# Dense attention in two-head groups with two-bank score tiles, instead of four-head groups with one-bank tiles

## The chip, the cores and the metric

One Trainium2 chip, all 8 of its cores. Every core runs the same program on its own batch element (one 2048 x 1024 slice of x). The time is the device time of the slowest core, in microseconds. There is no exchange between cores.

## What is computed

A transformer block in two halves, each wrapped in layer norms with a residual. The change touches only the first half, a dense (all keys) attention with 16 heads of 64 over 2048 tokens:

```python
def _L0_attn_ref(x, qkv_w, qkv_b, proj_w, proj_b):      # x: (8, 2048, 1024)
    qkv = einsum('bsd,ed->bse', x, qkv_w) + qkv_b        # 16 heads of 64
    scores = einsum('bhqe,bhke->bhqk', q, k) / sqrt(64)
    attn = softmax(scores, axis=-1)
    out = einsum('bhqk,bhke->bhqe', attn, v)
    return einsum('bsd,ed->bse', out, proj_w) + proj_b

x = x + layernorm(_L0_attn_ref(layernorm(x), ...))
x = x + layernorm(_L0_ffn_ref(layernorm(x), ...))       # two layers: windowed attention, gated FFN
```

The second half (two layers of windowed attention with rotary embedding and a gated feed-forward net) is the same before and after.

## The kernel before

The kernel is a chain of phases. Within a phase each engine has its instruction list in program order, written out by hand; a helper, `Phase.op`, attaches the semaphore waits. It adds one more wait to every VectorE instruction (for the VectorE instruction before it) and the same on ScalarE, so that neither engine ever overlaps two of its own instructions. A barrier stands between phases.

Phase D0 takes the layer-norm statistics, D1 makes the keys `kT` (bf16, head pair c on partitions 0-63 and 64-127) and the values `vTM` (bf16, keys on partitions, with a column of ones at index 64 that yields the softmax sums), D2 makes queries, attention and output projection. D2 runs four times, once for each block of 512 queries (`qb`). In each it computes the queries `qto` (L549, L554), a bound on each head's scores as the negative number to add before the exponential (L569 to L584), then the attention proper (L588 to L672), then the normalisation (L673 to L694), the projection (L699 to L724) and the statistics and residual (L729 to L788).

The attention proper, which is what the change rewrites, goes over four groups `cg` of two head pairs each (four heads). Of each group:

- L603 spreads the bound of each of the four heads over 128 partitions with a small matmul, L606 copies it to SBUF (`bnegb`, in the buffer that the profile calls sqbuf), one copy for each head.
- The loop `kc` runs over 16 chunks of 128 keys, and one step more. In step kc, L623 computes four score tiles (one for each head; 64 rows of the array each, 128 keys x 512 queries), each into its own PSUM bank 0 to 3; L630 adds the bound and writes `tmp2` (f32, one slot for each head); L637 takes the exponential into `pt` (bf16, two slots for each head, by the parity of kc). Then L653 multiplies the values of chunk ka = kc-1 with `pt`, four matmuls with 65 output rows, accumulated in PSUM banks 4 to 7.
- L661 to L670 evict the two sums and the two outputs of each head pair, eight VectorE instructions for the group.

Three waits matter. L623 waits for the add of the step before on its bank. L630 waits for the exponential of the step before on its `tmp2` slot. And L653 waits for `s_exp[bank]`: the dictionary holds the exponential last issued for that bank, and when L653 of chunk kc-1 is issued, step kc has overwritten it. So L653 of chunk kc-1 waits for the exponential of chunk kc. TensorE issues in order, so the score matmuls of step kc+1 stand behind those.

## Time and profile before

| | before |
|---|---|
| median of 2 runs | 5703.12 us (5676.47 to 5729.78) |
| profiled execution, its own time | 5702.29 us |
| its span, slowest core (core 5) | 5700.7 us |
| spans of the eight cores | 5654.3 to 5700.7 us |
| TensorE busy | 3448.1 us, 60% |
| VectorE busy | 2057.9 us, 36% |
| ScalarE busy | 1457.4 us, 26% |
| GpSimd busy | 200.3 us, 4% |

The span is the time from the first to the last instruction of the slowest core. Busy shares are means over the whole span, and phases differ much from one another; no engine is near full. A group of instructions is one source line on one engine: its busy time, the mean duration of one, and the idle time of that engine directly before them, with what ended it. The granted clock is the share of TensorE's full 2.4 GHz that was passed to it: 0.50 is 1.2 GHz.

### The profile page before, as it was taken

The page shows a single profiled execution, that of the slowest core. Times are in us where ns is not written, and L with a number is a line of the kernel's source. Part 1 is how long each engine was busy: PE and PEld are TensorE (multiplying, and loading weights), DVE is VectorE, ACT ScalarE, POOL GpSimd, SP SyncE. Part 2 cuts the span into 40 slices and gives each one's busy share as a digit, 9 for nine tenths or more (in the row PEclk, how much of TensorE's full clock was granted, in tenths as well). Part 3 has the DMA queues.
Part 4 walks back from the last instruction along what each step waited for, and adds up shares of the span by engine and source line. Part 5 has one row for each costly group of instructions (what it writes and reads, how often), then busy time and mean ns, then how long its engine had stood idle before and what let it go on. Part 6 is the DMA issues. An engine that isn't in the chain of part 4 may idle for free. (4 is left out here: it accounts for less than half of the span.)

```text
span 5700.7 us, 45607 instructions; the slowest of 8 cores (5654.3 to 5700.7 us)
## 1 busy us (share of the span) xinstructions
PE 3448.1 (60%) x10688; PEld 1058.7 (19%) x10688; DVE 2057.9 (36%) x2871; ACT 1457.4 (26%) x2325; POOL 200.3 (4%) x211
## 2 busy tenths in 40 slices
PE   2656664565466556641555756969654774788891
PEld 0211111111111111110111211424211111133330
DVE  2112553455255345534333334222033333322215
ACT  2222442343244334421122222111021221311211
POOL 0000000000000000000000000101000000011010
PEclk8786556555655555555666565989766556599895
DMA  3001001100300110022000000635600000045453
GB/s 91 1 0 19 1 1 16 15 1 1 30 1 1 15 15 1 1 70 59 1 1 1 1 1 12 79 41 73 99 0 0 1 1 0 8 59 63 54 62 118
DMA packets 268634, 143.96 MB, mean 25 GB/s; under 512 B 161728, under 2 KB 251968, under 8 KB 265312
## 3 DMA queue, kind: packets, MB, share of 16 engines
q0 software_dynamic: 256144, 107.27, 15.5%
q1 hardware_dynamic: 12240, 33.78, 1.7%
q8 instruction: 106, 1.74, 0.1%
q14 instruction: 144, 1.18, 0.1%
HBM read 222.99 MB, written 16.78 MB: 42 GB/s over the span
## 5 line engine op out<-in xcount | busy, mean ns | idle before, releaser
L630 DVE TENSOR_TENSOR tmp<-psD,sqbuf 128x512 f32<-128x512 f32 x1024 | 708.4, 692 | 626.9 <-PE psD L623 540.9
L653 PE MATMUL psD<-PTbuf,vTM 128*65 128x512 bf16 x1024 | 610.3, 609 | 497.9 <-ACT PTbuf L637 491.4
L637 ACT ACTIVATE PTbuf<-tmp 128x512 bf16<-128x512 f32 x1024 | 646.1, 631 | 823.6 <-DVE tmp L630 698.7
L1175 PE MATMUL psF<-xhat,w1b 128*128 128x512 bf16 x1408 | 341.5, 386 | 66.6 <-DVE xhat L1149 60.3
L623 PE MATMUL psD<-qTO,kT 64*128 64x512 bf16 x1024 | 306.2, 613 | 75.2 <-DVE sqbuf L606 61.1
L885 PE MATMUL psA<-castbuf,wkv 128*128 128x512 bf16 x768 | 256.2, 493 | 156.9 <-DVE castbuf L866 133.8
L1181 PE MATMUL psF<-xhat,w1b 128*128 128x512 bf16 x1408 | 336.9, 383 | 0.0
L1216 PE MATMUL psF<-Gbuf,w2b 128*128 128x512 bf16 x1408 | 325.5, 396 | 15.1 <-DVE Gbuf L1191 8.1
L653 PEld LDWEIGHTS psD<-PTbuf,vTM 128*65 128x65 bf16 x1024 | 136.6, 133 | 1055.1 <-issue 1055.0
L1191 DVE SCALAR_TENSOR_TENSOR Gbuf<-psF,s_b1i,gel 128x512 bf16<-128x512 f32 x176 | 132.1, 751 | 506.6 <-ACT gel L1188 506.6
L1022 ACT ACTIVATE PTA<-psA,s_cf 128x512 bf16<-128x512 f32 (+1 forms) x448 | 236.8, 528 | 287.1 <-PE psA L1010 269.7
L1005 PE MATMUL psA<-qv,kb 64*128 64x512 bf16 x448 | 270.7, 604 | 4.4 <-DVE vTMl L974 4.4
L1188 ACT ACTIVATE gel<-psF,s_b1i 128x512 bf16<-128x512 f32 x176 | 121.1, 688 | 484.5 <-PE psF L1181 484.5
L1046 PE MATMUL psA<-PTA,vTMl 128*65 128x512 bf16 x448 | 233.7, 631 | 12.1 <-DVE PTA L1029 7.3
L1029 DVE MEMSET PTA<- 128x128 bf16 (+1 forms) x336 | 91.3, 272 | 316.9 <-PE psA L1046 277.5
L1175 PEld LDWEIGHTS psF<-xhat,w1b 128*128 128x128 bf16 x1408 | 136.4, 99 | 245.4 <-issue 100.7
L1216 PEld LDWEIGHTS psF<-Gbuf,w2b 128*128 128x128 bf16 x1408 | 141.6, 101 | 199.0 <-issue 79.3
L1181 PEld LDWEIGHTS psF<-xhat,w1b 128*128 128x128 bf16 x1408 | 139.0, 99 | 170.5 <-issue 12.2
L68 POOL DMA_DIRECT2D w1b<-w1i x88 | 83.8, 953 | 2462.0 <-SPq L79 1749.8
L549 PE MATMUL psD<-castbuf,wQ 128*128 128x512 bf16 x256 | 83.1, 492 | 132.0 <-DVE castbuf L521 90.7
L1222 DVE SCALAR_TENSOR_TENSOR x_res<-psF,s_b,x_res 128x512 f32<-128x512 f32 x64 | 48.1, 752 | 288.6 <-PE psF L1216 288.6
L951 PE MATMUL psA<-u2b,c_rr 128*128 128x512 bf16 x64 | 37.5, 585 | 171.0 <-DVE u2b L949 171.0
(204 smaller groups left out, 2996.2 us busy)
## 6 DMA issues: line engine op xcount, KB each, us to landing
w1b<-w1i POOLq DMA_DIRECT2D x88, 512.0 KB, 6.0
w2b<-w2p POOLq DMA_DIRECT2D x32, 704.0 KB, 8.3
x_res<-xT SPq DMA_DIRECT2D x1, 8192.0 KB, 29.2
wQ<-wqT POOLq DMA_DIRECT2D x32, 256.0 KB, 4.5
wP<-projT POOLq DMA_DIRECT2D x32, 256.0 KB, 4.6
xsave<-x_res SPq DMA_DIRECT2D x1, 8192.0 KB, 25.3
xo<-xsave SPq DMA_DIRECT2D x4, 2048.0 KB, 12.7
yT<-tmpo SPq DMA_DIRECT2D x4, 2048.0 KB
```

The lines of the kernel that those rows point to most:

```text
L623: tmm = ph.op("tensor", lambda e, kc=kc, r0=r0, bank=bank, cc=cc: e.matmul(pb[:, bank, :], kT[r0:r0 + 64, cc, kc * 128:kc * 128 + 128], qt ...
L630: v_add[bank] = ph.op("vector", lambda e, bank=bank, bslot=bslot: e.tensor_tensor(tmp2[:, bank, :], pb[:, bank, :], bnegb[:, bslot, :], AL ...
L637: s_exp[bank] = ph.op("scalar", lambda e, slot=slot, bank=bank: e.activation(pt[:, slot, :], tmp2[:, bank, :], AF.Exp, scale=0.125), waits ...
L653: t_av[slot] = ph.op("tensor", lambda e, cc=cc, ka=ka, slot=slot, obank=obank, par_h=par_h: e.matmul(pb[0:65, obank, :], vTM[:, ka, 2 * cc ...
L885: tlast = ph.op("tensor", lambda e, ci=ci, par=par, co=co, sl=sl: e.matmul(pb[:, par, :], wkv[:, ci, co * 128:co * 128 + 128], sl, start=( ...
L1005: ph.op("tensor", lambda e, c=c, kt=kt, r0=r0, bank=bank: e.matmul(pb[:, bank, :], kb[r0:r0 + 64, c, kt * 128:kt * 128 + 128], qv[r0:r0 + ...
L1022: s_exp[bank] = ph.op("scalar", lambda e, bank=bank, e0=e0, e1=e1: e.activation(pt[:, bank, e0:e1], pb[:, bank, e0:e1], AF.Exp, bias=b.s_c ...
L1046: t_av[bank] = ph.op("tensor", lambda e, c=c, kt=kt_a, bank=bank, obank=obase + par_h, par_h=par_h, ka=ka, nk=nk: e.matmul(pb[0:65, obank, ...
L1175: tl_a = ph.op("tensor", lambda e, ci=ci, jp=jp, bA=bA, o=o: e.matmul(pb[:, bA, :], w1b[:, jp, ci, 0:128], xh[:, ci, o:o + QB], start=(ci ...
L1181: tl_g = ph.op("tensor", lambda e, ci=ci, jp=jp, bG=bG, o=o: e.matmul(pb[:, bG, :], w1b[:, jp, ci, 128:256], xh[:, ci, o:o + QB], start=(c ...
L1191: v_g[sg] = ph.op("vector", lambda e, bA=bA, j=j, o=o, s_g=s_g, sg=sg: e.scalar_tensor_tensor(G[:, j, o:o + QB], pb[:, bA, :], b.s_b1i[:, ...
L1216: tl = ph.op("tensor", lambda e, j=j, fp=fp, bank=bank, o=o: e.matmul(pb[:, bank, :], w2b[:, fp, j, :], G[:, j, o:o + QB], start=(j == 0), ...
```

## The change

The loops of the attention proper are rewritten; all that is around them stays. The group is now one head pair c (eight groups for a query block instead of four). A step `kg` takes two chunks of keys of both heads. The four PSUM score banks are now given by head and chunk (bank = 2*par_h + j2) and not by head alone; the four matmuls of a step are issued as head 0 chunk 0, head 0 chunk 1, head 1 chunk 0, head 1 chunk 1. One add and one exponential serve two banks, 128 x 1024 elements, with the bound broadcast over the two. The value matmuls of step kg-1 now wait for the exponentials recorded under step kg-1. Output banks are 4, 5 for even c and 6, 7 for odd c. A wait of `kg == 0` and the list that ScalarE waits for at L737 are written for the new names.

The core of the diff (the evictions and the normalisation that follow are the same statements with `cc` renamed to `c`):

```diff
@@ -587,89 +587,92 @@
                 inc="V")
             v_oev = None
             v_last_of_pair = {}
-            s_exp = {0: None, 1: None, 2: None, 3: None}
-            v_add = {0: None, 1: None, 2: None, 3: None}
-            v_bb = {0: None, 1: None, 2: None, 3: None}
+            s_expg = {}
+            v_addg = {}
+            v_bb = {}
             t_av = {i: 0 for i in range(8)}
-            for cg in range(4):
-                pairs = (2 * cg, 2 * cg + 1)
-                for cc in pairs:
-                    for par_h in range(2):
-                        h = 2 * cc + par_h
-                        bslot = (cc % 2) * 2 + par_h
-                        wts = [("V", v_bq)]
-                        if v_add[bslot] is not None:
-                            wts.append(("V", v_add[bslot]))
-                        t_s = ph.op("tensor", lambda e, h=h, bslot=bslot: e.matmul(
-                            pb[:, bslot, :], b.c_selh[:, h * 128:h * 128 + 128],
-                            bq16[:], start=True, stop=True), waits=wts, inc="T")
-                        v_bb[bslot] = ph.op("vector", lambda e, bslot=bslot: e.tensor_copy(
-                            bnegb[:, bslot, :], pb[:, bslot, :]), waits=[("T", t_s)], inc="V")
+            for c in range(8):
+                obase = 4 + 2 * (c % 2)
+                for par_h in range(2):
+                    h = 2 * c + par_h
+                    bslot = (c % 2) * 2 + par_h
+                    wts = [("V", v_bq)]
+                    if v_addg.get((7, par_h, c - 1)) is not None:
+                        wts.append(("V", v_addg[(7, par_h, c - 1)]))
+                    t_s = ph.op("tensor", lambda e, h=h, par_h=par_h: e.matmul(
+                        pb[:, par_h * 2, :], b.c_selh[:, h * 128:h * 128 + 128],
+                        bq16[:], start=True, stop=True), waits=wts, inc="T")
+                    v_bb[bslot] = ph.op("vector", lambda e, bslot=bslot, par_h=par_h: e.tensor_copy(
+                        bnegb[:, bslot, :], pb[:, par_h * 2, :]), waits=[("T", t_s)], inc="V")
                 t_avl = {}
-                for kc in range(17):
-                    if kc < 16:
-                        for cc in pairs:
-                            for par_h in range(2):
-                                bank = (cc % 2) * 2 + par_h
-                                bslot = bank
-                                r0 = 64 * par_h
+                for kg in range(9):
+                    if kg < 8:
+                        tsm = {}
+                        for par_h in range(2):
+                            for j2 in range(2):
+                                kc = 2 * kg + j2
+                                bank = par_h * 2 + j2
                                 waits = []
-                                if s_evq[0] is not None and kc == 0 and par_h == 0 and cc == pairs[0]:
+                                if s_evq[0] is not None and kg == 0 and par_h == 0 and j2 == 0:
                                     waits += [("S", s_evq[0]), ("S", s_evq[1])]
-                                if v_add[bank] is not None:
-                                    waits.append(("V", v_add[bank]))
-                                if kc == 0:
-                                    waits.append(("V", v_bb[bslot]))
-                                tmm = ph.op("tensor", lambda e, kc=kc, r0=r0, bank=bank, cc=cc: e.matmul(
-                                    pb[:, bank, :], kT[r0:r0 + 64, cc, kc * 128:kc * 128 + 128],
-                                    qto[r0:r0 + 64, cc, :], start=True, stop=True,
+                                prev_add = v_addg.get((kg - 1, par_h, c)) or v_addg.get((7, par_h, c - 1))
+                                if kg == 0:
+                                    waits.append(("V", v_bb[(c % 2) * 2 + par_h]))
+                                if prev_add is not None:
+                                    waits.append(("V", prev_add))
+                                tsm[par_h] = ph.op("tensor", lambda e, kc=kc, r0=64 * par_h, bank=bank, c=c: e.matmul(
+                                    pb[:, bank, :], kT[r0:r0 + 64, c, kc * 128:kc * 128 + 128],
+                                    qto[r0:r0 + 64, c, :], start=True, stop=True,
                                     tile_position=(r0, 0)), waits=waits, inc="T")
-                                aw2 = [("T", tmm)]
-                                if s_exp[bank] is not None:
-                                    aw2.append(("S", s_exp[bank]))
-                                v_add[bank] = ph.op("vector", lambda e, bank=bank, bslot=bslot: e.tensor_tensor(
-                                    tmp2[:, bank, :], pb[:, bank, :], bnegb[:, bslot, :],
-                                    ALU.add), waits=aw2, inc="V")
-                                slot = bank + 4 * (kc % 2)
-                                wts = [("V", v_add[bank])]
-                                if t_av[slot]:
-                                    wts.append(("T", t_av[slot]))
-                                s_exp[bank] = ph.op("scalar", lambda e, slot=slot, bank=bank: e.activation(
-                                    pt[:, slot, :], tmp2[:, bank, :], AF.Exp,
-                                    scale=0.125), waits=wts, inc="S")
-                    if kc >= 1:
-                        ka = kc - 1
-                        for cc in pairs:
-                            for par_h in range(2):
-                                bank = (cc % 2) * 2 + par_h
-                                obank = 4 + bank
-                                avw = [("S", s_exp[bank])]
+                        for par_h in range(2):
+                            bslot = (c % 2) * 2 + par_h
+                            aw = [("T", tsm[par_h])]
+                            prev_exp = s_expg.get((kg - 1, par_h, c)) or s_expg.get((7, par_h, c - 1))
+                            if prev_exp is not None:
+                                aw.append(("S", prev_exp))
+                            v_addg[(kg, par_h, c)] = ph.op("vector", lambda e, par_h=par_h, bslot=bslot: e.tensor_tensor(
+                                tmp2[:, par_h * 2:par_h * 2 + 2, :],
+                                pb[:, par_h * 2:par_h * 2 + 2, :],
+                                bnegb[:, bslot:bslot + 1, :].broadcast_to([128, 2, QB]),
+                                ALU.add), waits=aw, inc="V")
+                            ptbase = (kg % 2) * 4 + par_h * 2
+                            wts = [("V", v_addg[(kg, par_h, c)])]
+                            if t_av[ptbase] or t_av[ptbase + 1]:
+                                wts.append(("T", max(t_av[ptbase], t_av[ptbase + 1])))
+                            s_expg[(kg, par_h, c)] = ph.op("scalar", lambda e, par_h=par_h, ptbase=ptbase: e.activation(
+                                pt[:, ptbase:ptbase + 2, :], tmp2[:, par_h * 2:par_h * 2 + 2, :],
+                                AF.Exp, scale=0.125), waits=wts, inc="S")
+                    if kg >= 1:
+                        kga = kg - 1
+                        for par_h in range(2):
+                            for j2 in range(2):
+                                ka = 2 * kga + j2
+                                slot = (kga % 2) * 4 + par_h * 2 + j2
+                                obank = obase + par_h
+                                avw = [("S", s_expg[(kga, par_h, c)])]
                                 if ka == 0:
-                                    if v_last_of_pair.get(cc - 2) is not None:
-                                        avw.append(("V", v_last_of_pair[cc - 2]))
-                                    if cc % 2 == 1 and s_qn_prev and cg == 0:
+                                    if v_last_of_pair.get(c - 2) is not None:
+                                        avw.append(("V", v_last_of_pair[c - 2]))
+                                    if c == 1 and s_qn_prev:
                                         avw.append(("S", s_qn_prev))
-                                slot = bank + 4 * (ka % 2)
-                                t_av[slot] = ph.op("tensor", lambda e, cc=cc, ka=ka, slot=slot, obank=obank, par_h=par_h: e.matmul(
-                                    pb[0:65, obank, :], vTM[:, ka, 2 * cc + par_h, 0:65],
+                                t_av[slot] = ph.op("tensor", lambda e, c=c, ka=ka, slot=slot, obank=obank, par_h=par_h: e.matmul(
+                                    pb[0:65, obank, :], vTM[:, ka, 2 * c + par_h, 0:65],
                                     pt[:, slot, :], start=(ka == 0), stop=(ka == 15)),
                                     waits=avw, inc="T")
-                                t_avl[(cc, par_h)] = t_av[slot]
...
@@ -731,9 +734,10 @@
                 sqw2 = []
                 if c == 0:
                     sqw2 = [("S", s_att[0]), ("S", s_att[1])]
-                    for bk in range(4):
-                        if v_add[bk] is not None:
-                            sqw2.append(("V", v_add[bk]))
+                    for ph_ in range(2):
+                        la = v_addg.get((7, ph_, 7))
+                        if la is not None:
+                            sqw2.append(("V", la))
                 s_sq1 = ph.op("scalar", lambda e, c=c: e.activation(
                     b.sq[:, c, :], attb[:, c, :], AF.Square),
                     waits=sqw2, inc="S")
```

## Rows read from the trace of the kernel before

**Rows 1.** The page: busy share of two engines, and the TensorE clock in 40 slices.

```profile
PE 3448.1 (60%) x10688; PEld 1058.7 (19%) x10688; DVE 2057.9 (36%) x2871; ACT 1457.4 (26%) x2325; POOL 200.3 (4%) x211
PEclk8786556555655555555666565989766556599895
```

**Rows 2.** The page's groups: line, engine, shapes, count, busy us, mean ns, idle before.

```profile
L630 DVE TENSOR_TENSOR tmp<-psD,sqbuf 128x512 f32<-128x512 f32 x1024 | 708.4, 692 | 626.9 <-PE psD L623 540.9
L653 PE MATMUL psD<-PTbuf,vTM 128*65 128x512 bf16 x1024 | 610.3, 609 | 497.9 <-ACT PTbuf L637 491.4
L637 ACT ACTIVATE PTbuf<-tmp 128x512 bf16<-128x512 f32 x1024 | 646.1, 631 | 823.6 <-DVE tmp L630 698.7
```

**Rows 3.** Three lines of the first query block: count, duration ns, first and last start.

```profile
L603 PE MATMUL psD<-bq,c_selh x20: 581/629/629, 520.3 to 1033.9; 16*128 16x512 bf16 x20
L661 DVE CAST castbuf<-psD x8: 685/688/691, 610.3 to 898.0; 1x512 bf16<-1x512 f32 x8
L670 DVE CAST qTO<-psD x8: 683/685/685, 612.7 to 900.4; 64x512 bf16<-64x512 f32 x8
```

**Rows 4.** Timeline of one step kc, all engines: start us, duration us, idle before.

```profile
627.69 1.04 PE L623 MATMUL psD<-qTO,kT 64*128 64x512 bf16 x4
628.54 3.08 DVE L630 TENSOR_TENSOR tmp<-psD,sqbuf 128x512 f32<-128x512 f32 x4 [2.47 <-PE psD L623]
629.43 0.63 ACT L637 ACTIVATE PTbuf<-tmp 128x512 bf16<-128x512 f32 x1 [2.53 <-DVE tmp L630]
630.21 0.61 PE L653 MATMUL psD<-PTbuf,vTM 128*65 128x512 bf16 x1 [1.48 <-ACT PTbuf L637]
...
632.60 0.61 PE L653 MATMUL psD<-PTbuf,vTM 128*65 128x512 bf16 x1 [0.19 <-ACT PTbuf L637]
633.14 1.03 PE L623 MATMUL psD<-qTO,kT 64*128 64x512 bf16 x4
```

**Rows 5.** Timeline around the boundary between two groups, same columns.

```profile
605.06 3.08 DVE L630 TENSOR_TENSOR tmp<-psD,sqbuf 128x512 f32<-128x512 f32 x4 [2.65 <-PE psD L623]
609.12 2.31 PE L653 MATMUL psD<-PTbuf,vTM 128*65 128x512 bf16 x5 [0.18 <-ACT PTbuf L637]
610.33 0.69 DVE L661 CAST castbuf<-psD 1x512 bf16<-1x512 f32 x1 [2.19 <-PE psD L653]
616.63 3.07 DVE L606 CAST sqbuf<-psD 128x512 bf16<-128x512 f32 x4
617.46 0.58 PE L623 MATMUL psD<-qTO,kT 64*128 64x512 bf16 x1 [4.22 <-DVE sqbuf L606]
619.80 2.28 DVE L630 TENSOR_TENSOR tmp<-psD,sqbuf 128x512 f32<-128x512 f32 x3
620.64 0.58 PE L623 MATMUL psD<-qTO,kT 64*128 64x512 bf16 x1 [0.21 <-DVE tmp L630]
```

**Rows 6.** Groups by shape: how durations grow with the width; a full-clock matmul.

```profile
L783 DVE TENSOR_TENSOR x_res<-x_res,attb 128x4096 f32<-128x4096 f32 x4 | 17.7, 4427 | 0.4
L1022 ACT ACTIVATE PTA<-psA,s_cf 128x512 bf16<-128x512 f32 x112 | 77.1, 688 | 64.6 <-PE psA L1010 59.3
L1022 ACT ACTIVATE PTA<-psA,s_cf 128x384 bf16<-128x384 f32 x112 | 65.2, 582 | 75.1 <-PE psA L1010 65.2 <-ACT PTA L1022 7.8
L1175 PE MATMUL psF<-xhat,w1b 128*128 128x512 bf16 x1408 | 341.5, 386 | 66.6 <-DVE xhat L1149 60.3 <-DMA w1b<-w1i 6.1
L637 ACT ACT_TABLE_LOAD x4 | 5.1, 1283 | 22.4 <-DVE tmp L630 22.4
```

**Rows 7.** Windows, busy us (count) of PE, PEld, DVE, ACT, POOL, then PEclk, DMA share, GB/s.

```profile
520.00:611.00 91.00, 57.72 (x132) 11.72 (x132) 47.88 (x70) 41.66 (x65) 0.00 (x0) 0.50 0.00 1
3413.60:3417.00 3.40, 3.40 (x10) 0.70 (x8) 0.80 (x4) 1.77 (x3) 0.00 (x0) 0.50 0.00 0
480.00:482.00 2.00, 2.00 (x6) 0.76 (x5) 0.00 (x0) 0.00 (x0) 0.00 (x0) 0.50 0.00 0
482.00:484.00 2.00, 2.00 (x8) 0.74 (x6) 0.00 (x0) 1.89 (x2) 0.87 (x1) 0.72 0.00 0
```

More of the change, by code:

```diff
@@ L655, in phase_dense @@
                                     pt[:, slot, :], start=(ka == 0), stop=(ka == 15)),
                                     waits=avw, inc="T")
-                                t_avl[(cc, par_h)] = t_av[slot]
-                for cc in pairs:
-                    obase = 4 + (cc % 2) * 2
-                    h0, h1 = 2 * cc, 2 * cc + 1
-                    ph.op("vector", lambda e, h=h0, obase=obase: e.tensor_copy(
-                        sums[32 * (h // 4):32 * (h // 4) + 1, h % 4, :], pb[64:65, obase, :]),
-                        waits=[("T", t_avl[(cc, 0)])], inc="V")
-                    ph.op("vector", lambda e, h=h1, obase=obase: e.tensor_copy(
-                        sums[32 * (h // 4):32 * (h // 4) + 1, h % 4, :], pb[64:65, obase + 1, :]),
-                        waits=[("T", t_avl[(cc, 1)])], inc="V")
-                    ph.op("vector", lambda e, cc=cc, obase=obase: e.tensor_copy(
-                        qto[0:64, cc, :], pb[0:64, obase, :]),
-                        waits=([("Ld", l_tapq)] if (cc == 0 and l_tapq) else []), inc="V")
-                    v_oev = ph.op("vector", lambda e, cc=cc, obase=obase: e.tensor_copy(
-                        qto[64:128, cc, :], pb[0:64, obase + 1, :]), inc="V")
-                    v_last_of_pair[cc] = v_oev
@@ new lines, in phase_dense @@
+                                t_avl[par_h] = t_av[slot]
+                h0, h1 = 2 * c, 2 * c + 1
+                ph.op("vector", lambda e, h=h0, obase=obase: e.tensor_copy(
+                    sums[32 * (h // 4):32 * (h // 4) + 1, h % 4, :], pb[64:65, obase, :]),
+                    waits=[("T", t_avl[0])], inc="V")
+                ph.op("vector", lambda e, h=h1, obase=obase: e.tensor_copy(
+                    sums[32 * (h // 4):32 * (h // 4) + 1, h % 4, :], pb[64:65, obase + 1, :]),
+                    waits=[("T", t_avl[1])], inc="V")
@@ L673, in phase_dense @@
+                ph.op("vector", lambda e, c=c, obase=obase: e.tensor_copy(
+                    qto[0:64, c, :], pb[0:64, obase, :]),
+                    waits=([("Ld", l_tapq)] if (c == 0 and l_tapq) else []), inc="V")
+                v_oev = ph.op("vector", lambda e, c=c, obase=obase: e.tensor_copy(
+                    qto[64:128, c, :], pb[0:64, obase + 1, :]), inc="V")
+                v_last_of_pair[c] = v_oev
             l_sc = None
```

## The prediction

> **What bounds the kernel now.** I read the page first. No engine is full over the span, and the TensorE clock falls to 6 and 5 tenths from the fourth slice on [rows 1]. The costliest groups are the add, the exponential and the value matmul of the dense attention; each has nearly as much idle time before it as busy time, or more, and the three name each other as releasers: the add waits for the scores, the exponential for the add, the value matmul for the exponential [rows 2]. That is a loop in which the engines take turns. The chain that ended last says nothing here, since it only shows the output phase; a barrier closes D2, so what is saved inside it is saved at the end.
>
> How long the attention lasts: in the first query block it runs from the first L603 at 520.3 to the end of the last L670 at 900.4 + 0.7 = 901.1, so 380.8 us, and there are four such blocks. A group takes about 95 us: the first L661 starts at 610.3, and that of the last group 3.1 us before 898.0; (894.9 - 610.3)/3 = 94.9 [rows 3].
>
> One step kc of the timeline is 633.14 - 627.69 = 5.45 us [rows 4]. Its parts: scores to first add 0.85; four adds in series 3.08; add to exponential 0.20 (the first add ends at 628.54 + 0.69 = 629.23, the exponential starts at 629.43); exponential 0.63; exponential to value matmul 0.15 (630.06 to 630.21); last value matmul to the next scores 0.54. Sum 5.45. TensorE, VectorE and ScalarE all lie on this one chain, because L653 of chunk kc-1 waits for the exponential of chunk kc and the next scores are queued behind it. No engine's own work sets the step: VectorE needs 4 x 0.795 = 3.2, ScalarE 4 x 0.80 = 3.2.
>
> **The change, part by part.** *The wait.* L653 of step kg-1 now waits for its own exponential, issued a step earlier. The loop is cut, and the step becomes the longest of three: VectorE's work, the chain of one head through its `tmp2` slot, and TensorE's queue. The work of a step is as before: 4 score tiles and 4 value matmuls, 256 steps in all.
>
> *Wide adds.* The row nearest to 128x1024 f32 on VectorE is 128x4096 f32, 4427 ns; against 692 for 512 the slope is (4427-692)/3584 = 1.042 ns an element, so 692 + 534 = 1.23 us [rows 2, 6]. Bounds: 1.23, and 2 x 692 = 1.38 if nothing of the fixed part is saved or the broadcast costs something. I take 1.23. Adds follow each other 0.10 apart (3.08 = 3 x 0.795 + 0.69) [rows 4], so VectorE needs 2 x 1.33 = 2.66 a step.
>
> *Wide exponentials.* ScalarE's slope is (688-582)/128 = 0.83 ns an element [rows 6], so 631 + 425 = 1.06 us; upper bound 2 x 631 = 1.26. Chain of one head: add 1.23, 0.20, exponential 1.06, 0.20 back = 2.68.
>
> *TensorE at half clock.* Matmuls in a row follow at (2.31-0.61)/4 = 0.425 us [rows 5]. The four scores of a step end 1.04 after their start = 0.425 + 0.61: two slots for four, because the heads alternate between the two halves of the rows and run in pairs [rows 4]. The new order is head 0, 0, 1, 1, so only the middle two can overlap: three slots, 1.28, where they are free to, four slots, 1.70, where not. Each change between score and value matmuls costs 0.54 - 0.425 = 0.11 more. The head-0 pair lets its add start 0.425 + 0.85 = 1.27 after the pair starts. The add of head 1 then ends at 1.27 + 1.23 + 0.10 + 1.23 = 3.82, and the head-1 scores of the next step may start 0.15 later (620.49 to 620.64 [rows 5]), at 3.97. With a step of length c they start 3.97 - c into it, and behind them come 0.85 (scores), 1.70 (values) and 0.22 (two changes): c = 3.97 - c + 2.77, c = 3.37, the head-1 scores starting at 0.60, in part beside the second head-0 tile. The exponentials are there in time. So TensorE's queue, at 1.2 GHz, is the longest of the three: 3.37 against 2.68 and 2.66. With no overlap of scores at all it would be 0.85 + 0.85 + 1.70 + 0.22 = 3.62.
>
> A page speaks against the new order: the Trainium skill, "TensorE: Matmul & The Clock Gate", Part 3, says that matmuls run concurrently where their tiles use different row groups. The trace agrees (1.04 us for four). By that rule the old order keeps TensorE's floor at two slots; the sum stays the one above, because it lets only the middle two overlap.
>
> *A head pair.* From the first add: first step 2.68 (nothing but scores is queued then); the second 4.06 (its head-1 scores start at 2.70, then 0.85, 0.11, values 1.70, 0.11 = 5.47, + 1.27 = 6.74 for the third add); five steps of 3.37 = 16.85; two last adds 2.55. Sum 26.14.
>
> *The boundary* comes 8 times a block instead of 4, for two heads. From the end of the last add: 0.20, exponential 1.06, 0.15, two value matmuls 0.425 + 0.61, 0.20: L664 starts at 2.65 (L661 went before). L664, L667, L670 take 0.795 each, the copy of the bound starts at 5.04 and ends at 5.73, then 0.15 and 1.27: the next add at 7.14. Before it was 608.14 (605.06 + 3.08) to 619.80 = 11.7 for four heads [rows 5]; now 14.3 for four. That is a loss of 2.6 for every old group, inside the sum below.
>
> *A query block.* 8 x 26.14 = 209.1; 7 x 7.14 = 50.0; start 0.63 + 0.20 + 0.69 + 0.15 + 1.27 = 2.9; end 2.65 + 2 x 0.795 + 0.69 = 4.9; the table load of the exponential, 1.3 [rows 6], which stands before the first exponential as it did. Sum 268.2 against 380.8: 112.6 less, in four blocks 450. The profiled execution took 5702.3, which is the median of the runs (5703.1) within 1 us; 5702 - 450 = 5252, say **5250 us**. Queries, normalisation, projection and all later phases keep their instructions and waits; their weight transfers are issued by GpSimd on TensorE's progress, not on anything that moves.
>
> **The unknown costs as ends.** No overlap of scores: + 0.25 x 5 x 32 = + 40. Widest add and exponential: the head-1 add ends 0.31 later, c = 3.53, + 0.16 x 5, first two steps + 0.6, last adds + 0.3, boundary + 0.2: about 1.9 x 32 = + 60. Steady steps at TensorE's own floor, 1.28 + 1.70 + 0.22 = 3.20: - 27. So this case alone runs from 5220 to 5315.
>
> **Rivals.**
> *The clock comes up.* In the attention before, TensorE had a matmul in flight 57.7 of 91 us and was granted 0.50 throughout [rows 7]. After the change it streams almost without a gap in a step. If it is granted 2.4 GHz, a slot is half as long, a matmul takes about 0.39 [rows 6], and the step falls to the chain, 2.68: a head pair 7 x 2.68 + 2.55 = 21.3, a boundary 0.86 less, 6.28, a block 8 x 21.3 + 7 x 6.28 + 8.2 = 222.6, the kernel 5702 - 4 x 158.2 = 5069. For it: the 128-row, 128-column matmuls that fill 480 to 484 run at 0.50 and then 0.72, so the clock rose to 1.00 within the second stretch [rows 7]. Against it: the windowed attention, whose matmuls have the same 64 rows or 65 columns, fills 3.40 of 3.40 us and stays at 0.50 (the row shown; 25 of 30 such stretches I read are full, all 30 at 0.50) [rows 7]. And a step of 2.68 at full clock leaves gaps, which may cost the clock again: then the time lies between 5069 and 5250. The same page, Part 1, says that sustained activity releases the throttle; by that rule this rival would win. The window at 3413.6 does not bear it out for matmuls that use half of the array. 0.20.
> *No decoupling.* If the value matmuls still ended up behind the exponential of the same step, the step would be 1.27 + 2.55 + 0.20 + 1.06 + 0.15 + 0.85 + 0.11 = 6.19: two wide instructions in series hide less than four narrow ones. A head pair with its boundary: 7 x 6.19 + 2.55 + 7.14 = 53.0 against 47.4, + 5.6 x 32 = + 180, 5880 us: slower. The point from which it decides is a step of about 5.4. The key of the new wait speaks against it: it names the step before. 0.03.
> *Wide instructions far above their slope* (the broadcast, or two banks in one read). VectorE would bound the step; at an add of 1.9 us the step is 4.0, a head pair 7 x 4.0 + 3.9 = 31.9, 5.8 above the 26.14, and the time 5250 + 32 x 5.8 = 5435. No row shows such an operand; the steady 692 for 512 from PSUM and the 4427 speak against it. 0.05.
>
> **How the numbers follow.** Half-clock case 0.72, clock up (wholly or in part) 0.20, wide instructions slow 0.05, no decoupling 0.03. Predicted 5250. The range takes in the half-clock case with its bounds and reaches down to the full-clock time: 5060 to 5315; the half-clock case alone is 5220 to 5315. A change of 2% is 114 us, about what a measurement of this kernel can tell from none; all but the third rival are beyond it on the fast side: faster 0.96, within 2% 0.01, slower 0.03.
>
> **What would show it.** Right: the add's group 512 times at about 1.23 us, the exponential at 1.06; clock 0.50 through D2's attention; score matmuls of a step about 3.4 us from the next, TensorE with almost no idle before the value matmuls; the blocks 268 us long. Wrong: a clock above 0.50 there; a step near 2.7 (clock) or 3.6 (overlap); idle before the value matmuls that still names the exponential; a boundary far from 7.1 us; or phases after D2 that change.

## The result, and the profile after

| | before | after |
|---|---|---|
| median of the runs | 5734.19 us (10 runs, 5676.47 to 5884.31) | 5177.57 us (11 runs, 5126.79 to 5256.57) |
| profiled execution | 5702.29 us | 5128.56 us |
| ratio to before | | 0.9054, 95% interval 0.8997 to 0.9111 |

The changed kernel is 9.5% faster. The forecast of 5250 us was 121 us above the profiled execution, and the range of 5060 to 5315 holds it. In some executions of either kernel the cores of one die run at a lower clock and take longer; the medians hold them, the ratio and the comparisons below do not.

The page after, busy share of the engines and the TensorE clock in 40 slices [rows 1], and the groups that answer to [rows 2]:

```profile
PE 3202.0 (62%) x10688; PEld 1060.0 (21%) x10688; DVE 1976.8 (39%) x2359; ACT 1353.1 (26%) x1813; POOL 200.3 (4%) x211
PEclk8777776776877775666656589797565665797995
L633 DVE TENSOR_TENSOR tmp<-psD,sqbuf 128x1024 f32<-128x1024 f32 x512 | 627.1, 1225 | 134.5 <-PE psD L623 74.6
L642 ACT ACTIVATE PTbuf<-tmp 128x1024 bf16<-128x1024 f32 x512 | 541.5, 1058 | 382.7 <-DVE tmp L633 358.1
L623 PE MATMUL psD<-qTO,kT 64*128 64x512 bf16 x1024 | 350.7, 472 | 191.4 <-DVE tmp L633 106.3
L658 PE MATMUL psD<-PTbuf,vTM 128*65 128x512 bf16 x1024 | 347.5, 439 | 66.0 <-ACT PTbuf L642 48.7
```

The idle time before the add fell from 626.9 to 134.5 us, that before the value matmul from 497.9 to 66.0. And the clock line, 6 and 5 through the attention before, now shows mostly 7, with some 6 and 8: the value matmul's mean is 439 ns where it was 609.

The first query block after, as in [rows 3] (count, duration ns, first and last start):

```profile
L602 PE MATMUL psD<-bq,c_selh x16: 374/384/629, 527.0 to 735.7; 16*128 16x512 bf16 x16
...
L673 DVE CAST qTO<-psD x8: 683/684/685, 556.7 to 767.8; 64x512 bf16<-64x512 f32 x8
```

A block lasts 768.5 - 527.0 = 241.5 us; the four last 241.5, 239.0, 237.7 and 240.4, where they were 380.8, 381.7, 379.5 and 382.2. That is 566 of the 574 us by which the two profiled executions differ. A head pair takes (767.8 - 556.7)/7 = 30.2 us: the output evictions of the first and of the eighth pair start seven pairs apart, and the pairs of the other runs are taken in the same way. The gain lies where the change is; all other phases together account for 8 us.

The timeline of one pair after (TensorE), its first steps at half clock, then a step at full clock:

```profile
591.80 1.01 PE L623 MATMUL psD<-qTO,kT 64*128 64x512 bf16 x2 [0.82 <-DVE tmp L633]
593.13 1.01 PE L623 MATMUL psD<-qTO,kT 64*128 64x512 bf16 x2 [0.32 <-DVE tmp L633]
594.07 1.92 PE L658 MATMUL psD<-PTbuf,vTM 128*65 128x512 bf16 x4
595.92 0.92 PE L623 MATMUL psD<-qTO,kT 64*128 64x512 bf16 x4
...
601.56 0.60 PE L623 MATMUL psD<-qTO,kT 64*128 64x512 bf16 x2
602.44 0.59 PE L623 MATMUL psD<-qTO,kT 64*128 64x512 bf16 x2 [0.27 <-DVE tmp L633]
602.96 1.33 PE L658 MATMUL psD<-PTbuf,vTM 128*65 128x512 bf16 x4
604.22 0.60 PE L623 MATMUL psD<-qTO,kT 64*128 64x512 bf16 x2
```

and the windows of the same pair (busy us of PE, PEld, DVE, ACT, POOL, then PEclk, DMA share, GB/s):

```profile
588.50:595.50 7.00, 5.19 (x12) 1.36 (x12) 5.88 (x6) 3.10 (x3) 0.00 (x0) 0.50 0.00 0
597.50:615.50 18.00, 13.08 (x48) 3.90 (x46) 14.99 (x14) 12.69 (x12) 0.00 (x0) 1.00 0.00 0
616.00:619.00 3.00, 0.22 (x1) 0.12 (x2) 2.59 (x5) 0.00 (x0) 0.00 (x0) 0.68 0.00 0
```

The step from 591.80 to 595.92 is 4.12 us, at half clock; the one from 601.56 to 604.22 is 2.66, VectorE's two adds. On this core each of the 32 pairs begins at 0.50 and rises to 1.00 later: 7 to 11 us after its first scores, in one pair only after 16. All but the last pair of a block have lost it again by the first scores of the next pair, most of them in the gap at the boundary. In 6 of the 32 pairs the clock also falls once inside the pair and comes back. One of these, beside the same place of the pair above (598.45), which stayed at 1.00:

```profile
598.45 0.59 PE L623 MATMUL psD<-qTO,kT 64*128 64x512 bf16 x2 [0.63 <-DVE tmp L633]
599.78 0.59 PE L623 MATMUL psD<-qTO,kT 64*128 64x512 bf16 x2 [0.74 <-DVE tmp L633]
...
687.13 0.59 PE L623 MATMUL psD<-qTO,kT 64*128 64x512 bf16 x2 [0.63 <-DVE tmp L633]
688.46 0.76 PE L623 MATMUL psD<-qTO,kT 64*128 64x512 bf16 x2 [0.74 <-DVE tmp L633]
689.00:692.00 3.00, 3.00 (x9) 0.80 (x8) 1.87 (x2) 2.46 (x3) 0.00 (x0) 0.50 0.00 0
```

The idle times before the two places are the same, so they alone do not decide.

### The profile page after: what moved, and what is told of

Same layout as the page of the kernel before. It is cut to its first block and busy times, and to the rows that moved or that the text cites. A ratio compares the mean times of both kernels' runs of the same rounds, so it can differ in the third digit from the quotient of the medians.

```text
span 5126.8 us, 41631 instructions; the slowest of 8 cores (5087.5 to 5126.8 us)
## 1 busy us (share of the span) xinstructions
PE 3202.0 (62%) x10688; PEld 1060.0 (21%) x10688; DVE 1976.8 (39%) x2359; ACT 1353.1 (26%) x1813; POOL 200.3 (4%) x211
## 5 line engine op out<-in xcount | busy, mean ns | idle before, releaser
L633 DVE TENSOR_TENSOR tmp<-psD,sqbuf 128x1024 f32<-128x1024 f32 x512 | 627.1, 1225 | 134.5 <-PE psD L623 74.6
L642 ACT ACTIVATE PTbuf<-tmp 128x1024 bf16<-128x1024 f32 x512 | 541.5, 1058 | 382.7 <-DVE tmp L633 358.1
L623 PE MATMUL psD<-qTO,kT 64*128 64x512 bf16 x1024 | 350.7, 472 | 191.4 <-DVE tmp L633 106.3
L658 PE MATMUL psD<-PTbuf,vTM 128*65 128x512 bf16 x1024 | 347.5, 439 | 66.0 <-ACT PTbuf L642 48.7
L1220 PE MATMUL psF<-Gbuf,w2b 128*128 128x512 bf16 x1408 | 312.1, 384 | 18.2 <-DMA w2b<-w2p 13.9
L623 PEld LDWEIGHTS psD<-qTO,kT 64*128 64x128 bf16 x1024 | 80.5, 97 | 447.5 <-issue 430.7
L658 PEld LDWEIGHTS psD<-PTbuf,vTM 128*65 128x65 bf16 x1024 | 104.8, 121 | 300.2 <-issue 291.4
```

The lines of the kernel that those rows point to most:

```text
L623: tsm[par_h] = ph.op("tensor", lambda e, kc=kc, r0=64 * par_h, bank=bank, c=c: e.matmul(pb[:, bank, :], kT[r0:r0 + 64, c, kc * 128:kc * 12 ...
L633: v_addg[(kg, par_h, c)] = ph.op("vector", lambda e, par_h=par_h, bslot=bslot: e.tensor_tensor(tmp2[:, par_h * 2:par_h * 2 + 2, :], pb[:, ...
L642: s_expg[(kg, par_h, c)] = ph.op("scalar", lambda e, par_h=par_h, ptbase=ptbase: e.activation(pt[:, ptbase:ptbase + 2, :], tmp2[:, par_h * ...
L658: t_av[slot] = ph.op("tensor", lambda e, c=c, ka=ka, slot=slot, obank=obank, par_h=par_h: e.matmul(pb[0:65, obank, :], vTM[:, ka, 2 * c + ...
L1220: tl = ph.op("tensor", lambda e, j=j, fp=fp, bank=bank, o=o: e.matmul(pb[:, bank, :], w2b[:, fp, j, :], G[:, j, o:o + QB], start=(j == 0), ...
```

## The experiments

Two theories. A: the gain is that of the wait, the value matmuls no longer stand behind the exponential of a later chunk. B: it is that of the wide instructions and of the two-bank tiles. The first two runs are the other two corners of that square.

**e1_own_wait**: the kernel before, with A alone.

```diff
+                                s_own[(kc, bank)] = s_exp[bank]
...
-                                avw = [("S", s_exp[bank])]
+                                avw = [("S", s_own[(ka, bank)])]
```

> The kernel before with one edit: the value matmuls wait for the exponential of their own chunk, not for the one of the chunk after; narrow adds and exponentials, four heads in a group. Theory A (the wait is the cause): the step falls from 5.45 us to VectorE's 4 x 0.795 = 3.2; from the first add of a group to the end of the last 16 x 3.18 = 50.9, with the old boundary of 11.7 a group takes 62.6 instead of 94.9, so 16 x 32.3 = 517 us less, about 5185. Theory B (the gain comes from the wide instructions and the two-bank tiles): within 50 us of the kernel before. On the clock: TensorE would need 2.77 of 3.18 us a step at half clock; if a stream that is denser than before is what raises the clock, it leaves 0.50 here too, without changing the time much.

Measured: 5138.8 us in the profiled execution and 5152.1 in another; the profiled execution of the changed kernel took 5128.6. So the wait alone brings 564 of the 574 us. It is 46 us under the expected 5185: a group takes 60.5 us (worked out under e10_four_heads_wide) and not 62.6. Its groups and its windows:

```profile
L631 DVE TENSOR_TENSOR tmp<-psD,sqbuf 128x512 f32<-128x512 f32 x1024 | 708.6, 692 | 111.3 <-ACT PTbuf L638 4.2
L655 PE MATMUL psD<-PTbuf,vTM 128*65 128x512 bf16 x1024 | 311.6, 422 | 22.1 <-ACT PTbuf L638 22.0
```

```profile
594.00:596.00 2.00, 2.00 (x7) 0.49 (x5) 1.79 (x3) 1.65 (x3) 0.00 (x0) 0.50 0.00 0
596.00:598.00 2.00, 2.00 (x7) 0.66 (x5) 1.62 (x4) 1.50 (x3) 0.00 (x0) 0.50 0.01 4
598.00:600.00 2.00, 1.58 (x7) 0.38 (x6) 1.79 (x3) 1.60 (x3) 0.00 (x0) 0.93 0.00 0
```

The busy time of the add is what it was (708.4 then), the idle time before it went from 626.9 to 111.3. VectorE is busy 1.6 to 1.8 of every 2 us at either clock: here the clock rises too (0.50, then 0.93), but does not set the step. The step is 3.18 us as expected, four narrow adds.

**e2_wide_old_wait**: the changed kernel with the old wait put back, so B alone.

```diff
-                                avw = [("S", s_expg[(kga, par_h, c)])]
+                                avw = [("S", s_expg[(min(kg, 7), par_h, c)])]
```

> The changed kernel with one edit: the value matmuls of step kg-1 wait for the exponential of step kg, as before the change. Theory A: the step is 1.27 + 2.55 + 0.20 + 1.06 + 0.15 + 0.85 + 0.11 = 6.19 us at half clock, a head pair 53 us, the kernel about 180 us slower than before, 5880; clock 0.50 in the attention. Theory B (wide instructions bring the gain): clearly faster than before, below 5500.

Measured: 5818.7 to 5825.2 us, ratio to before 1.0229 (1.0209 to 1.0249): slower than before. One step, all engines:

```profile
605.97 1.04 PE L623 MATMUL psD<-qTO,kT 64*128 64x512 bf16 x4
607.25 2.55 DVE L633 TENSOR_TENSOR tmp<-psD,sqbuf 128x1024 f32<-128x1024 f32 x2 [3.75 <-PE psD L623]
608.68 1.06 ACT L642 ACTIVATE PTbuf<-tmp 128x1024 bf16<-128x1024 f32 x1 [3.82 <-DVE tmp L633]
609.88 1.04 PE L658 MATMUL psD<-PTbuf,vTM 128*65 128x512 bf16 x2 [2.87 <-ACT PTbuf L642]
610.01 1.06 ACT L642 ACTIVATE PTbuf<-tmp 128x1024 bf16<-128x1024 f32 x1 [0.27 <-DVE tmp L633]
611.21 1.03 PE L658 MATMUL psD<-PTbuf,vTM 128*65 128x512 bf16 x2 [0.29 <-ACT PTbuf L642]
612.17 1.04 PE L623 MATMUL psD<-qTO,kT 64*128 64x512 bf16 x4
```

612.17 - 605.97 = 6.20 us, where 6.19 was worked out. Theory B falls: wide instructions on a chain on which the engines take turns make it longer, since each successor waits for a larger piece. The same work, four score tiles and four value matmuls, took 5.45 us before [rows 4]. The time is 60 us under the expected 5880. The first step of a pair has only scores in front of it and takes 2.62 us instead of 6.19, but the drain at the end of the pair is longer than was summed; a pair comes to some 51.4 us instead of 53.0, which is 51 of the 60.

**e3_alternate**: the changed kernel with the scores in the order of before.

```diff
-                        for par_h in range(2):
-                            for j2 in range(2):
+                        for j2 in range(2):
+                            for par_h in range(2):
                                 kc = 2 * kg + j2
```

> The changed kernel with the four score matmuls of a step in the order of before (head 0, head 1, head 0, head 1), which run in pairs. By the chain of waits: no add can start before both adds of the step before are done and all scores but one are through, so a step is 1.27 + 2.55 + 0.15 = 3.97 us at half clock and about 3.4 at full clock, against 2.7 to 3.4 now: 25 to 35 percent of slack lost in each step, 5330 to 5370 us. By the rule that pairs in different row groups save TensorE time: not slower than the changed kernel, 5128 to 5177.

Measured: 5310.4 to 5332.0 us, ratio 0.9347 (0.9321 to 0.9373). TensorE's timeline and a window of the same stretch:

```profile
606.58 0.60 PE L623 MATMUL psD<-qTO,kT 64*128 64x512 bf16 x1
607.45 1.01 PE L623 MATMUL psD<-qTO,kT 64*128 64x512 bf16 x3 [0.26 <-DVE tmp L633]
608.38 1.92 PE L658 MATMUL psD<-PTbuf,vTM 128*65 128x512 bf16 x4
610.24 0.60 PE L623 MATMUL psD<-qTO,kT 64*128 64x512 bf16 x1
```

```profile
608.00:612.00 4.00, 3.74 (x11) 0.96 (x8) 2.45 (x2) 2.46 (x3) 0.00 (x0) 0.50 0.00 0
```

One score goes out, then the three others wait for the second add. The step is 610.24 - 606.58 = 3.66 us, some 0.3 less than the 3.97 of the expectation, which gave the first score tile of the step no head start. About 190 us are lost by an order that keeps every pairing of row halves. The rule on row groups does not decide here; which tiles an add waits for does.

The clock is lower too: 0.50 in all 14 windows of 4 us that I read from 600 to 656, with TensorE in flight (a matmul running, by the records) 3.74 of 4.00 us in the steady ones. But it is not always there: in 9 of the 32 pairs of this core it rises for a while later in the pair. One such step:

```profile
694.59 0.66 PE L623 MATMUL psD<-qTO,kT 64*128 64x512 bf16 x3 [0.26 <-DVE tmp L633]
698.03 0.66 PE L623 MATMUL psD<-qTO,kT 64*128 64x512 bf16 x3 [0.96 <-DVE tmp L633]
```

From 694 to 698 the granted clock is 0.97, and the step is 3.44 us (3.4 was worked out), against 2.66 in the changed kernel at full clock. So of the 1.0 us that a steady step is longer, about 0.8 is there at full clock too and is the order's; some 0.2 comes with the lower clock.

**e6_filler**: the clock, held up in the boundary.

```diff
+                if c >= 1:
+                    for fi in range(12):
...
+                        ph.op("tensor", lambda e, obase=obase, c=c: e.matmul(
+                            pb[:, obase, :], kT[:, c, 0:128], kT[:, c, 0:512],
+                            start=True, stop=True), waits=fw)
```

> The changed kernel with 12 extra full-array matmuls (128x128x512, results never used) on TensorE in each boundary between head pairs, into the output banks that are free then. They fill the 2.95 us in which TensorE waits for the copy of the bound. Theory: the clock falls in that gap and comes back only some 7 us later, and the steps in between take about 3.3 us instead of 2.66. With the gap filled the clock stays at 1.00 through the block, each of the 28 inner pairs takes 27.6 instead of 30.2 us, 70 us less, about 5060 in the profiled execution. Rival: the clock is decided by something else (work of other engines, current), then no change or a little slower by the filler.

Measured: 5099.0 and 5103.7 us in two executions, 5160.0 and 5169.2 in two others. By the lowest of each it is some 28 us less than the changed kernel (5126.8 and 5128.6); the ratio to before is 0.9018 (0.8938 to 0.9097), whose interval overlaps that of the changed kernel. A pair takes (754.5 - 547.2)/7 = 29.6 us. Windows over one boundary (604 to 610) and what follows:

```profile
604.00:610.00 6.00, 4.73 (x20) 1.65 (x18) 5.18 (x7) 0.52 (x1) 0.00 (x0) 1.00 0.01 3
613.00:618.00 5.00, 5.00 (x13) 1.27 (x12) 3.24 (x4) 3.36 (x4) 0.00 (x0) 0.50 0.00 0
621.00:630.00 9.00, 7.28 (x27) 2.14 (x26) 8.00 (x8) 6.67 (x8) 0.00 (x0) 1.00 0.00 1
```

The filler kept 1.00 through the boundary; the clock then fell all the same, inside the pair, after its first step, in which TensorE has scores only and waits for adds (0.82 and 0.74 us idle before them). It does so in the first steps of 21 of the 28 inner pairs of this core. So the gap at the boundary was only one of the places where the clock goes, and I had named it as the only one; the expected 70 us came to 28.

The stretch at half clock shows what the timeline of the changed kernel above does not, full steps in a row that TensorE bounds:

```profile
612.67 1.74 PE L633 MATMUL psD<-qTO,kT 64*128 64x512 bf16 x4
616.19 1.47 PE L633 MATMUL psD<-qTO,kT 64*128 64x512 bf16 x4
619.43 1.33 PE L633 MATMUL psD<-qTO,kT 64*128 64x512 bf16 x4
```

They take 3.52 and 3.24 us, 3.38 in the mean, where the prediction had 3.37 for a steady step.

**e4_pipelined** takes the boundary itself away: the bound of the next pair is made in the middle of the running one, and the next pair's first scores, adds and exponentials are issued before the last value matmuls and the evictions.

```diff
+                    if kg == 4 and c < 7:
+                        bound(c + 1)
...
+                    if kga == 7:
+                        evict(ca)
```

> The changed kernel with the boundary between head pairs taken out of the chain: the bound of the next pair is made in the middle of the running pair (matmul into the free output banks, copy on VectorE), and the scores, adds and exponentials of the next pair's first step are issued before the evictions of the last. VectorE then never waits for a drained pipeline: a pair is its work, 16 x 1.33 + 6 x 0.795 = 26.05 us, a block 8 x 26.05 + 9 = 217 us against 240 now, four blocks 90 us less, about 5040 in a profiled execution. TensorE has no gap of some 3 us any more, so theory says that the clock, once up, stays at 1.00 to the end of the block. Rival: the clock falls all the same and TensorE's queue (3.37 a step at half clock) holds a pair at 27 us, block 225, 5070. If neither the gap nor the boundary mattered: 5128, as now.

Measured: 5078.0 to 5110.9 us, ratio 0.8899 (0.8802 to 0.8996); a pair (757.3 - 561.0)/7 = 28.0 us, not 26.05. The profiled execution is 51 us under that of the changed kernel; 90 was expected. Where the rest is:

```profile
617.29 0.68 DVE L623 CAST qTO<-psD 64x512 bf16<-64x512 f32 x1
618.08 0.69 DVE L625 CAST qTO<-psD 64x512 bf16<-64x512 f32 x1
618.87 5.21 DVE L655 TENSOR_TENSOR tmp<-psD,sqbuf 128x1024 f32<-128x1024 f32 x4
620.24 1.01 PE L643 MATMUL psD<-qTO,kT 64*128 64x512 bf16 x2 [2.42 <-DVE tmp L655]
```

The evictions now stand between two adds on VectorE, TensorE waits 2.42 us for the add behind them, and the clock is at 0.50 after it (the matmuls last 1.01 for two again). The rival of the expectation held: the clock falls all the same, and the time is 5078, near its 5070.

**e9_split**: as e4_pipelined, with the two bounds and the two outputs of a pair copied by ScalarE.

```diff
-                    v_bb[bslot] = ph.op("vector", lambda e, bslot=bslot, sb_=sb_: e.tensor_copy(
-                        bnegb[:, bslot, :], pb[:, sb_, :]), waits=[("T", t_s)], inc="V")
+                    v_bb[bslot] = ("S", ph.op("scalar", lambda e, bslot=bslot, sb_=sb_: e.activation(
+                        bnegb[:, bslot, :], pb[:, sb_, :], AF.Copy), waits=[("T", t_s)], inc="S"))
...
-                ph.op("vector", lambda e, c=c, obase=obase: e.tensor_copy(
+                ph.op("scalar", lambda e, c=c, obase=obase: e.activation(
```

> As e4_pipelined, and four of the six small copies of a pair (the two bounds and the two outputs) move from VectorE to ScalarE. VectorE 16 x 1.33 + 2 x 0.795 = 22.9 us a pair, ScalarE 16 x 1.23 + 4 x 0.86 = 23.1 us; a block 8 x 23.1 + 9 = 194, four blocks 183 us less than now, about 4945. If VectorE is not what bounds the steps (a head's chain through its slot of tmp2 does, 2.68 a step, and the copies delay that chain wherever they stand), the pair stays at 26 and the time at e4_pipelined's.

Measured: 5024.3 to 5032.3 us in three executions, 5084.0 in a fourth; ratio 0.8824 (0.868 to 0.897). A pair (733.2 - 555.6)/7 = 25.4 us, 2.6 less than in e4_pipelined. Work on VectorE was what bounded it. 4945 was too low: a pair is 2.3 us above the 23.1 of the sum. The clock still falls once or twice in most pairs (0.50 from 609.5 to 615.5 in one of them), which no run separates from other causes.

**e14_wide_over_heads**: the wide instruction lies over the two heads of one chunk.

```diff
-                                bank = par_h * 2 + j2
+                                bank = j2 * 2 + par_h
...
-                                bnegb[:, bslot:bslot + 1, :].broadcast_to([128, 2, QB]),
+                                bnegb[:, bslot:bslot + 2, :],
```

> The changed kernel with one add and one exponential over the two heads of one chunk, instead of over two chunks of one head. The scores are issued head 0, head 1 of the first chunk, then of the second, and each add waits for one such pair only; the pair runs at the same time in the two halves of the array, one slot instead of two before the first add can start. Widths and counts are the same, the bound needs no broadcast. At full clock VectorE bounds the step either way (2.66). At half clock the first add starts 0.85 us after its scores instead of 1.27, so a step is (0.85 + 2.55 + 0.15 + 0.43 + 1.70 + 0.22)/2 = 2.95 at the least instead of 3.37; some three steps a pair run at half clock, and each boundary is 0.4 shorter: (3 x 0.42 + 0.43) x 32 = 54 us less than the changed kernel. If the order of the scores did not matter once all are released: the boundary alone, 14 us.

**after_again** is the measure beside it:

> The changed kernel itself, unedited, on the same chip as the three others, as the measure for them: 5128 to 5180.

Measured: after_again 5128.4 and 5134.9 us; e14_wide_over_heads 5114.1 us at the lowest, ratio to before 0.9009 (0.8894 to 0.9124). The median of cores 0 to 3 takes 5090 to 5102 us over five executions, that of after_again 5117 to 5123 over four: some 20 us less. The boundary alone was worked out at 14, the whole at 54. The likely reason for the miss, not tested: I had taken three half-clock steps a pair to be bound by TensorE, and the timeline of after shows one, which starts at 591.80, before the clock rises.

**e10_four_heads_wide**: e1_own_wait, and wide over the two heads of a pair. It has the width without the second set of boundaries.

```diff
+                            va = ph.op("vector", lambda e, b0=b0: e.tensor_tensor(
+                                tmp2[:, b0:b0 + 2, :], pb[:, b0:b0 + 2, :], bnegb[:, b0:b0 + 2, :],
+                                ALU.add), waits=aw2, inc="V")
```

> e1_own_wait (four heads in a group, 4 boundaries a block, value matmuls wait for their own exponential) with adds and exponentials made wide over the two heads of a pair. It has what the change gains by width without what it loses by twice the boundaries. Against e1_own_wait: 16 steps of 2.66 instead of 3.18 us at full clock, 2.95 at half; a group 3 x 2.95 + 13 x 2.66 + 11.5 = 55 instead of 60.5, 16 groups 88 us less, about 5050. If the wide instructions have no value by themselves: 5140, as e1_own_wait.

Measured: 5027.2 to 5042.4 us, ratio 0.8812 (0.875 to 0.8874). A group of four heads takes (740.3 - 3.15 - 576.2)/3 = 53.7 us, where 3.15 is the distance between the evictions of its two pairs; in e1_own_wait (767.5 - 3.15 - 582.8)/3 = 60.5; in the changed kernel 2 x 30.2 = 60.4. So the width is worth about 100 us once the wait is right, and the change gives all of it back. e14_wide_over_heads has the same wait, width and order and only the smaller groups: its lowest is 5114.1 against 5027.2, some 85 us for four more boundaries a block. The rest, some 15 to 20 us, is what e14 gains on the change by its order.

**e13_split_over_heads**: e9_split with the wide instructions over the heads.

> e9_split with the wide instructions over the two heads of a chunk, as in e14_wide_over_heads. e9_split took 5027 in its profiled execution; the half-clock steps shrink by 0.4 us, three a pair, 32 pairs: about 4985. If the steps are bound by VectorE and ScalarE alone there: 5027.

Measured: 4987.0 to 4995.1 us in three executions (5040.0 in a fourth), ratio 0.8756 (0.869 to 0.8823): the fastest of all, 12.4% under before. A pair (728.2 - 556.7)/7 = 24.5 us, 0.9 less than in e9_split, and the time is 37 us less where 42 was expected: here too the order over the heads pays. Its groups:

```profile
L655 DVE TENSOR_TENSOR tmp<-psD,sqbuf 128x1024 f32<-128x1024 f32 x512 | 627.1, 1225 | 131.7 <-PE psD L643 54.9 <-ACT PTbuf L664 18.6 <-ACT sqbuf L610 11.8
L664 ACT ACTIVATE PTbuf<-tmp 128x1024 bf16<-128x1024 f32 x512 | 541.2, 1057 | 169.9 <-DVE tmp L655 124.7 <-PE psD L681 37.0 <-PE psD L643 2.2
```

ScalarE's idle time before its exponentials is down from 382.7 to 169.9 us: it now carries four of the six copies.

## Why the prediction was right, and where not

*The bound of before* was right. One wait, L653 for the exponential of the next chunk, tied three engines into one chain. e1_own_wait cuts that wait alone and gets 5138.8 of the 5702.3; e2_wide_old_wait restores it in the new kernel and gets 5818.7.

*Wide instructions.* 1.23 and 1.06 us were worked out, 1225 and 1058 ns measured; the broadcast costs nothing. The third rival is out.

*The chains.* The step with the old wait: 6.19 worked out, 6.20 measured. From the first add of a pair to its third at half clock: 6.74 worked out, 597.08 - 590.43 = 6.65 measured. VectorE's step: 2.66, measured 2.66. The boundary: 7.14 at half clock and 6.28 at full clock; the adds of one pair end at 583.71 and the next begin at 590.43, 6.72, as a boundary has it that starts at full clock and ends at half:

```profile
581.15 2.56 DVE L633 TENSOR_TENSOR tmp<-psD,sqbuf 128x1024 f32<-128x1024 f32 x2
589.18 1.80 PE L623 MATMUL psD<-qTO,kT 64*128 64x512 bf16 x4 [2.95 <-DVE sqbuf L605]
590.43 5.21 DVE L633 TENSOR_TENSOR tmp<-psD,sqbuf 128x1024 f32<-128x1024 f32 x4 [0.71 <-PE psD L623]
597.08 7.88 DVE L633 TENSOR_TENSOR tmp<-psD,sqbuf 128x1024 f32<-128x1024 f32 x6 [1.44 <-PE psD L623]
```

*The step that failed* is "TensorE's queue, at 1.2 GHz, is the longest of the three". The case to which I gave 0.72 has the clock at 0.50 through the attention, five steps of 3.37 a pair, 268 us a block, 5250. In its place the rival of 0.20 came, in its partial form: the clock comes up in each pair after 7 to 11 us and goes at the boundary at the latest. A pair is 30.2 us, between 33.3 (half clock) and 27.6 (full clock); a block 240, between 268 and 223; the time 5129, between 5250 and 5069. The steady 3.37 us steps do not occur in the timeline of the changed kernel above. Their size was right (3.38 in e6_filler), what was wrong is that the clock stays where they occur. What misled me is the windowed attention, in flight 3.40 of 3.40 us at 0.50 with matmuls of the same half-filled array [rows 7] (between them, 128x128 mask matmuls on the full array, L1010); I took it as evidence that such matmuls don't raise the clock. e1_own_wait and the changed kernel show that they can. The Trainium skill, "TensorE: Matmul & The Clock Gate", Part 1, says that activity releases the throttle. The trace of after agrees: from 594.07 four value matmuls and the four scores behind them follow without a wait at half clock (1.92 us and 0.92), and from 602.96 four value matmuls last 1.33. The windowed attention does not agree: in flight throughout, it stays at 0.50.

So the time lay in the range for another reason than the one I held most likely. The range reached down to the full-clock time, and the partial rise of the clock was one of the rivals, at 0.20; the forecast of 5250 itself came from the case that failed.

*A second term* was wrong without consequence: that scores in the order head 0, 0, 1, 1 take three slots. In e2_wide_old_wait the four end 1.04 us after their start, as in [rows 4], in the new order. Where all four are released at once the order costs no slot. In the steady steps they are not released at once, so the sum of 3.37 came out near the 3.38 of e6_filler all the same.

*The boundary's loss* was priced somewhat high, 2.6 us for every old group at half clock against 2 x 6.72 - 11.7 = 1.7 for the one shown, but I did not ask what it does together with the width. The predicted sum hid that the wide instructions bring about 100 us and the change takes as much back: e10_four_heads_wide against e1_own_wait shows the one, e14_wide_over_heads against e10_four_heads_wide that some 85 of it are the doubled boundaries with their clock loss.

Not settled: what exactly decides when the clock rises and falls. The windowed attention, in flight throughout by the records, stays at 0.50, and e3_alternate, in flight 3.74 of 4 us, stays there for most of its pairs; e1_own_wait and the changed kernel rise. The same idle times are followed by 1.00 in one pair of the changed kernel and by 0.50 in another. The runs do not separate gaps from the kind of matmul.

## What to carry to other kernels

When three engines each sit idle before the others' work for about as long as they are busy, look for one wait that is a step too late; a dictionary overwritten between issue and use gives just that, and its repair costs no instruction. Wide instructions pay only when the engines already overlap: before that they lengthen the chain, and if they double the number of drained boundaries they give their gain back. A boundary between groups costs its own latency and then the clock of the next steps, so widen without adding boundaries (four more a block cost some 85 us here), or take the boundary out of the chain (51 us here).

## What the runs showed of the hardware

- A stream of half-array matmuls (64 rows, or 65 columns) can bring the clock to 1.00: in the changed kernel 7 to 11 us after a pair's first scores, in one pair after 16. Not every such stream does: the windowed attention, in flight 3.40 of 3.40 us [rows 7], stayed at 0.50.
- In the pair shown it stayed at 1.00 while VectorE bounded the step and TensorE was in flight 13.08 of 18 us. It was lost around a boundary with 2.95 us of idle TensorE. With that gap filled (e6_filler) it passed the boundary at 1.00 and was lost after a step with idle times of 0.82 and 0.74 us. Idle times of 0.63 and 0.74 us were followed by 1.00 in one pair of the changed kernel and by 0.50 in another.
- With 3.74 of 4.00 us in flight and one wait of 0.26 us in each step (e3_alternate) it stayed at 0.50 through 23 of 32 pairs and rose for a while in the 9 others.
- Four 64-row matmuls, two for each half of the rows, take 1.04 us at half clock whether they are issued alternating ([rows 4]) or two and two (e2_wide_old_wait), where all four are released at once.
- A 128x1024 f32 add from two PSUM banks with its second operand broadcast over them takes 1225 ns, the same as with two separate operands (1225 in e10_four_heads_wide).
